# A compressed interaction network on one core: ScalarE's queue issues the seven small loads of layer 0's last tile, SyncE's queue the rest

## The reference

```python
h = inputs                                             # [B, 39, 16]
for i in range(3):
    x = jnp.einsum('bhd,bmd->bhmd', h, inputs)         # every h row times every field
    x = x.reshape(B, -1, EMB_DIM)                      # 39*39, then 100*39 rows
    x = jnp.einsum('bcd,oc->bod', x, Ws[i]) + bs[i][None, :, None]
    x = jax.nn.relu(x)                                 # 200 outputs
    if i != n_layers - 1:
        h, direct = (x[:, :size // 2], x[:, size // 2:])
    else:
        direct = x
    finals.append(direct)
cin_result = jnp.sum(jnp.concatenate(finals, axis=1), axis=-1)
```

## Time and profile before

| | |
|---|---|
| median of 3 runs | 2736.91 us (2735.3 to 2737.49) |
| the profiled execution | 2729.3 us, span 2727.4 us |
| PE busy | 2621.5 us (96%) |
| DVE busy | 2280.7 us (84%) |
| ACT busy | 1815.4 us (67%) |
| POOL busy | 2312.9 us (85%) |
| DMA moved | 361.80 MB, mean 133 GB/s |

### The profile page before, as it was taken

One profiled execution on the slowest core, in us unless ns is written; L12 is line 12 of the kernel. 1 busy time (PEld: TensorE's weight loads), 2 busy tenths in 40 slices (PEclk: granted clock), 3 DMA queues, 4 the chain that ended last, 5 costly groups with the idle time before them and its releaser, 6 DMA issues.

```text
span 2727.4 us, 68845 instructions
## 1 busy us (share of the span) xinstructions
PE 2621.5 (96%) x17790; PEld 2616.0 (96%) x17790; DVE 2280.7 (84%) x4622; ACT 1815.4 (67%) x4784; POOL 2312.9 (85%) x2168
## 2 busy tenths in 40 slices
PE   0599999999999999999999999999999999999998
PEld 0599999999999999999999999999999999999998
DVE  3688888888888888888888888888888888888885
ACT  0567676666667767677676676667676676777763
POOL 5799888988989888898888889899898988877763
PEclk9799999999999999999999999999999999999999
DMA  8854555545545454554545545454554545545431
GB/s 150 199 135 125 141 131 132 137 116 139 141 129 140 122 149 127 132 137 123 151 122 137 132 122 153 121 139 129 134 145 119 144 125 142 138 121 138 123 113 55
DMA packets 249865, 361.80 MB, mean 133 GB/s; under 512 B 69531, under 2 KB 167362, under 8 KB 249538
## 3 DMA queue, kind: packets, MB, share of 16 engines
q1 hardware_dynamic: 235570, 354.51, 48.5%
q0 software_dynamic: 10496, 2.88, 2.7%
q10 hardware_dynamic: 3600, 2.73, 0.3%
HBM read 356.02 MB, written 14.17 MB: 136 GB/s over the span
## 4 chain that ended last, share of the span: by engine, by line
PE 94%; POOL 2%; SPq 2%; issue 1%; DVE 1%; DMA 1%; ACT 0%; POOLq 0%; DVEq 0%; ACTq 0%
PE acc L676 61%; PE acc L677 28%; PE acc L702 2%; POOL raw L522 1%; PE hrep L713 1%; SPq L390 0%; DVE W L1135 0%; DMA odd<-lin 0%; SPq L333 0%; SPq L323 0%; DMA raw<-table,idx 0%; PE acc L778 0%; PE acc L777 0%; PE acc L779 0%; POOL xlo_p L581 0%
## 5 line engine op out<-in xcount | busy, mean ns | idle before, releaser
L676 PE MATMUL acc<-W,xhi_d 128*128 128x400 f32 x5632 | 1730.6, 367 | 17.2 <-DVE xlo_d L1161 10.5
L677 PE MATMUL acc<-W,xlo_d 128*128 128x200 f32 x5632 | 1434.5, 255 | 0.0
L1153 DVE TENSOR_TENSOR prod_d<-hrep,xrep 128x512 f32<-128x512 f32 (+1 forms) x1536 | 1038.6, 676 | 121.4 <-issue 31.5
L1161 DVE TENSOR_TENSOR xlo_d<-prod_d,xhi_d 128x512 fp32r<-128x512 f32 (+1 forms) x1536 | 983.0, 640 | 182.6 <-ACT xhi_d L862 147.1
L677 PEld LDWEIGHTS acc<-W,xlo_d 128*128 128x128 f32 x5632 | 1077.7, 191 | 0.0
L676 PEld LDWEIGHTS acc<-W,xhi_d 128*128 128x128 f32 x5632 | 1058.9, 188 | 19.3 <-DVE xlo_d L1161 12.1
L581 POOL TENSOR_TENSOR xlo_p<-prod_p,xhi_p 128x512 fp32r<-128x512 f32 (+1 forms) x768 | 921.3, 1200 | 87.8 <-ACT xhi_p L856 57.3
L862 ACT ACTIVATE xhi_d<-prod_d 128x512 fp32r<-128x512 f32 (+1 forms) x1536 | 879.8, 577 | 163.9 <-PE acc L677 142.2
L676 PE MATMUL acc<-W,xhi_p 128*128 128x400 f32 x2816 | 881.5, 363 | 15.3 <-POOL xlo_p L581 15.3
L570 POOL TENSOR_TENSOR prod_p<-hrep_s,xrep 128x512 f32<-128x512 f32 x512 | 666.0, 1301 | 91.9 <-ACT hrep_s L899 50.9
L677 PE MATMUL acc<-W,xlo_p 128*128 128x200 f32 x2816 | 720.4, 256 | 0.0
(11 more groups left out here) (110 smaller groups left out, 1193.0 us busy)
## 6 DMA issues: line engine op xcount, KB each, us to landing
xrep<-xs SPq DMA_DIRECT2D x384, 384.0 KB
xrep<-xs SPq DMA_DIRECT2D x384, 128.0 KB
xrep<-xs SPq DMA_DIRECT2D x128, 336.0 KB
l0x<-xs SPq DMA_DIRECT2D x504, 80.0 KB
l0x<-xs SPq DMA_DIRECT2D x252, 63.0 KB
l0x<-xs SPq DMA_DIRECT2D x882, 7.0 KB
xrep<-xs SPq DMA_DIRECT2D x128, 64.0 KB
l0x<-xs SPq DMA_DIRECT2D x126, 64.0 KB
```

The source lines that it names most:

```text
L676: pe.matmul(bank[:, 0:2 * OUTS], hi, w, start=first, stop=last, skip_group_check=True)
L677: return pe.matmul(bank[:, 0:OUTS], lo, w[:, 0:OUTS], start=False, stop=last, skip_group_check=True)
L1153: nc.vector.tensor_tensor(to, h, xrep[:, (par + layer - 1) % 2, a:a + count, :], ALU.mult).then_inc(s_prod_d, 1)
L1161: op = nc.vector.tensor_tensor(xlo_d[:, slot, 0:split], bank[:, 0:split], xhi_d[:, slot, 0:split].bitcast(F32), ALU.subtract)
```

## The change

The seven loads of 14 rows for the last tile of layer 0 leave `load_layer0` and become a function `load_last_tile(engine, c)`. SP still issues them for chunk 2, ahead of the loop. In the steps, ACT issues them for chunk i+2 on its own queue, right behind the high of P1. Addresses, sizes and the semaphore stay as they were; ACT has waited for P1's products there, as SP has for its own seven.

```diff
--- before.py
+++ after.py
@@ -324,6 +324,16 @@
                                  src[QUARTER * q:QUARTER * q + used - full * QUARTER, full, :]).then_inc(
                                      s_lin[layer], 16)
 
+        def load_last_tile(engine, c):
+
+            for at, slot, field, step in [(at, KT[0] - 1, A_MAIN + L0_WHOLE, P) for at in (0, QUARTER, L0_LOW)] + [
+                    (0, KT[0] + 2, A_MAIN, 0), (QUARTER, KT[0] + 2, A_MAIN, 0), (L0_LOW, KT[0] + 2, A_MAIN, 0),
+                    (L0_LOW, KT[0] + 3, A_MAIN, 0)]:
+                x = xs[bass.ds(c, 1), field:field + 1, :].rearrange("c m n -> (c m n)")
+                engine.dma_start(l0x[at:at + 2 * A_REST, slot, :],
+                                 bass.AP(tensor=x.tensor, offset=x.offset,
+                                         ap=[[step, 2], [P, A_REST], [1, P]])).then_inc(s_l0x, 16)
+
         def load_weights(engine, layer, src):
             engine.wait_ge(s_lin[layer], 16 * LIN_DMAS[layer])
             to, rest = raw_weights(layer, 0, ODD), odd[layer]
@@ -395,10 +405,6 @@
                     load(A_MAIN * j, A_MAIN, slice(0, L0_MAIN), L0_MAIN * j, [[P, A_MAIN], [1, L0_MAIN * P]])
                 for step, slot in ((P, L0_MAIN), (0, KT[0] + 1)):
                     load(0, L0_WHOLE * A_REST, slice(slot, slot + 1), A_MAIN, [[step, L0_WHOLE], [P, A_REST], [1, P]])
-                for at in (0, QUARTER, L0_LOW):
-                    load(at, 2 * A_REST, slice(KT[0] - 1, KT[0]), A_MAIN + L0_WHOLE, [[P, 2], [P, A_REST], [1, P]])
-                for at, slot in ((0, KT[0] + 2), (QUARTER, KT[0] + 2), (L0_LOW, KT[0] + 2), (L0_LOW, KT[0] + 3)):
-                    load(at, 2 * A_REST, slice(slot, slot + 1), A_MAIN, [[0, 2], [P, A_REST], [1, P]])
 
             def load_block(c, buf, e):
 
@@ -456,6 +462,7 @@
             sp.wait_ge(s_pt, 6)
             sp.wait_ge(s_prod_p, p_num(0, 1) + 1)
             load_layer0(2)
+            load_last_tile(sp, 2)
             for e in (1, 2, 0, 3):
                 sp.wait_ge(s_xblk[e], BLOCK_SEM[e])
                 load_block(1, 1, e)
@@ -915,6 +922,9 @@
                         high(i, kind, g)
                     elif g != p_groups[-1]:
                         high(i, kind, g + 1)
+                        if g == 0 and (not isinstance(i, int) or i + 2 <= LAST):
+
+                            load_last_tile(act, i + 2)
                     elif 1 in layers and 2 in present(i + 1):
                         high(i + 1, kind, p_groups_of(i + 1)[0])
                     if isinstance(i, int) and i == 1 and kind == "D" and g in W2_AT:
```

## The result

The changed kernel takes 2999.09 us (median of 5 runs, 2997.33 to 3004.40) against 2735.30 us before (5 runs, 2732.77 to 2737.49) on the same chip. The ratio is 1.097, its 95% interval 1.0958 to 1.0982: slower by 264 us. The forecast was 2880 us, 143 us more than the 2737 us that it started from. It is in the range, but the mechanism that it describes makes up only about half of the loss, and the range owes its upper end to dearer issues and a longer hand-over, not to what made up the other half. The profiled execution took 2997.33 us, its span is 2995.5 us and TensorE's mean granted clock in it 0.97.

What follows compares the result with a forecast made beforehand. PE was taken to bound the kernel at 20.01 us a step. A loop through DVE and ACT, 14.4 + 0.7 + 5.3 + 0.75 = 21.15 us, adds 1.14 us in 125 steps, 143 us: 2880 us, range 2770 to 3020.

Steps and rivals of the forecast that it cites:

- dearer issues and a longer hand-over: Upper end of the range: 0.85 us per ACT issue and 1.2 us hand-over give 22.3 us a step, 3023 us.
- SP's relief: SP's queue issues seven loads fewer a step; claimed worth 0, at most the loop's one stall, 2.5 us in all.
- An issue blocks ACT: ACT's queue behind P1's high: issuing holds ACT, but the first DMA waits only for that high's waits, not its execution.
- Seven issues: ACT's seven small loads a step, taken at 0.76 us each, 5.3 us in all.
- The 0.12 us for two queues at once: Extra time per issue when SP and ACT issue together, from SP's load: 0.71 us beside ACT's, 0.59 us alone.
- DVE's loop: From D0's low through DVE's dot, ACT's issues and D0's high to the next: 21.15 us against PE's 20.01; chance 0.80.
- DVE's hole: DVE stands still ahead of D0's low, waiting for ACT's late D0 high: 3.5 us a step.
- What is late next: P2's high and POOL's low of P2 come some 4 us late; POOL's idle time just suffices, nothing added.
- The signs for DVE's loop alone: In the loop: PE busy 94 to 96%, P1's last matmuls 21 to 21.3 us apart, PE waiting before D0.
- The sign for POOL's loop: PE's wait standing in front of a P group would mean that POOL's loop binds, not DVE's.
- the hole closes in time: PE's step leaves 4.16 us for ACT's loads, 0.59 us each; the time stays at 2737 us; chance 0.11.
- the queues take turns: ACT's and SP's issues exclude each other; ACT's seven last up to 9.96 us, total time up to 3462 us; chance 0.07.

## Why the prediction was right or wrong

- **PE bounds the kernel before; SP's relief is worth nothing.** Right: with the loads off SP and one at a time on ACT the ratio is 1.0000.
- **An issue blocks ACT, but its sequencer runs ahead of the engine.** Right: the first DMA starts 0.17 us into P1's high.
- **Seven issues, 5.3 us at 0.76 each.** This term was too large: the blocks take 4.95 us (median of 125), 0.70 each. The 0.12 us for two queues at once did not come on ACT's side: all 875 of ACT's took 0.613 to 0.736 us, SP's own seven of this form 0.610 us:

```profile
L333 ACTq DMA_DIRECT2D l0x<-xs x875: 613/615/736, 108.3 to 2874.2; - x175
...
L333 SPq DMA_DIRECT2D l0x<-xs x7: 609/610/685, 89.4 to 93.4; - x7
```

- **DVE's loop, 21.15 us, 143 us in all.** Right in place and nearly in size: 20.97 us a step, seen once the gathers are out of POOL's way. PE's wait is in front of D0, DVE's hole is 3.45 us. That the loss of that kernel, 139 us, lies so near 143 us is in part luck: DVE's loop alone costs some 120 us, and POOL's scaling of each new tile, 19 us, makes up most of the difference.
- **"What is late next ... POOL has 16 to 20 us idle in 160 ..., just enough; I add nothing."** This is the step that failed. It put at nothing a loop that costs about half of the 264 us, and it is why the time came out 119 us above the forecast. It compared a delay with an average of idle time. Its own numbers were not even enough: low of P2 some 4 us later, against 2.0 to 2.5 and 1.1 us. POOL's idle time is not where the delay arrives either: from the low of P2 on POOL works nearly without a pause up to the product of P1, for which ACT's block of the next step waits. DVE's way was added up as a loop, POOL's wasn't. The same sum from rows gives 22.65 us. That the time is in the range all the same, 21 us below its end, is luck: that end stood for issues of 0.85 us and a hand-over of 1.2 us, and neither came.
- **The signs for DVE's loop alone.** P1's last matmuls were to be 21 to 21.3 us apart: that came in the steps with two gathers, while those with three take 22.6 us. PE was to be busy for 94 to 96% of a window: it was for 93 to 94%.
- **The sign for POOL's loop.** I wrote that PE would then wait in front of a P group. It waits in front of D0 all the same (172.1 us in 126 waits), since ACT's D0 high is behind the same block that waits for POOL. The engine in front of which PE stands doesn't name the loop; that the step's length follows the gathers does.
- **The rival "the hole closes in time"** needed 0.59 us an issue; they take 0.70. The room it named, 4.16 us, was nearly right: DVE's loop without the block is 20.97 less 4.93, 16.04 us, which leaves 3.97 us, and five loads in 3.52 us do fit (20.01 us in the steps with two gathers).
- **The rival "the queues take turns"** is excluded as it was priced, with ACT's seven lasting up to 9.96 us: ACT's rows would have been long where SP's stand beside them, and half of all are within 2 ns of the shortest. SP is the one that pays, and little. Its seven remaining loads, before the change and after:

```profile
1306.15 4.64 SPq L390 DMA_DIRECT2D l0x<-xs  x7
...
1332.56 5.15 SPq L400 DMA_DIRECT2D l0x<-xs  x7
```

By the median of all steps they take 4.61 us before and 5.01 us after, 0.4 us more. The Trainium skill's rule (Perfetto Trace Analysis, DMA Instruction - HWDGE (DVE, Sync)) is that descriptor generation is locked for one sequencer at a time, with the wait for the lock in an issue's profiled time. ACT's rows show no such wait; SP's may, and no run tells what lengthens them.

## What to carry to other kernels

A block of DMA issues in an engine's queue is one long instruction. Don't price it by that engine's idle share: for each engine that waits for something behind the block, add up the whole way round from the block's own release through that engine to the block's next release, everything queued there included, work of other kinds too (here gathers). The longest such loop is the new step. Look as well at what the block stands behind, since it starts only when the waits ahead of it are over. If issues must move to an engine that computes, put them one at a time behind instructions that run anyway: the same seven loads cost 264 us in a block and nothing spread.

## What the runs showed of the hardware

- The time of an issue on ACT is steady, 613 to 736 ns over 875 of them, also with SP issuing beside it. What two queues at once cost shows on SP: 5.01 us for the seven loads that took 4.61 us alone (the forecast's subtraction gave 4.85).
- TensorE's granted clock falls behind PE's longer holes. Four windows of 4 us after the change (columns as in the windows above):

```profile
1624.00:1628.00 4.00, 2.40 (x17) 2.16 (x16) 0.14 (x1) 0.77 (x2) 2.58 (x4) 1.00 0.45 130
1628.00:1632.00 4.00, 3.40 (x14) 3.38 (x15) 3.83 (x7) 3.93 (x12) 2.58 (x2) 0.64 0.04 10
...
1648.00:1652.00 4.00, 3.22 (x23) 2.97 (x22) 1.50 (x3) 2.16 (x5) 2.20 (x3) 1.00 0.27 80
1652.00:1656.00 4.00, 4.00 (x29) 3.86 (x28) 3.72 (x9) 3.93 (x13) 3.27 (x3) 1.00 0.00 0
```

After a hole of 2.2 us the granted clock is 0.64 in the next window, part of it at the lower of the two levels (1.2 GHz); after one of 0.8 us it stays at 1.00 (2.4 GHz). Not every long hole is followed by a fall: after that of 2.1 us at 1717 us the clock stays up. PE's busy time is 2726.8 us in place of 2621.5, yet this cost little here, because PE wasn't what set the pace. PE's own marks alternate, the last matmul of P1 at

```profile
1609.16 0.27 PE L709 MATMUL acc<-W,xhi_p 128*128 128x200 f32 x1
...
1633.20 0.28 PE L709 MATMUL acc<-W,xhi_p 128*128 128x200 f32 x1
...
1654.38 0.28 PE L709 MATMUL acc<-W,xhi_p 128*128 128x200 f32 x1
```

24.04 and 21.18 us, while POOL's marks are 22.6 us apart in both: the slow stretch makes PE late and so the next hole short, and the sum, 45.22 us, is twice 22.61. Who reads the length of a step from PE's rows alone sees a noise that isn't there.
